# A two-layer adaptive feed-forward kernel: shared output tiles behind the expert blocks, weights in a ring of 14 slots, residual sums in the feed-forward

## The reference

```python
# layer 0: mix the channels of each batch element by a matrix chosen by its condition
xt = einsum('bct,bcd->bdt', x, W[condition])
# router: softmax scores over 16 experts, best 2 of 4 groups, top 2 experts -> gate
for e in 16 experts:   # width 128
    y += gate[e] * ((silu(xt @ ew1 + eb1) * (xt @ ew2 + eb2)) @ ew3 + eb3)
z = (silu(xt @ sw1 + sb1) * (xt @ sw2 + sb2)) @ sw3 + sb3      # shared expert, width 256
x = x + y + z
# layer 1: causal convolution of each channel with a kernel made from state-space parameters, masked by length
u = conv(x * mask, K) + x * mask * D,  masked again
h = relu(u @ up_w) ** 2
f = h @ down_w + ((u @ fc1_w) @ expert_w * (sum of top 2 of u @ gate_w)) @ fc2_w
x = x + layernorm(f) * gamma + beta
```

## Time and profile before

| | us |
|---|---|
| median of 3 runs | 416.92 |
| lowest, highest | 415.62, 421.37 |
| profiled execution, its own time | 415.92 |
| its span, first to last instruction | 413.9 |
| PE busy in it (1883 matmuls) | 343.5 |
| DVE, ACT, POOL busy | 182.1, 119.7, 93.7 |

### The profile page before, as it was taken

How to read it: one execution, slowest core, us unless ns; L and a number is a source line. 1 busy time by engine, 2 the same in 40 slices (tenths; PEclk the granted TensorE clock), 3 DMA queues, 4 the chain that set the end, 5 groups by cost and what they waited for, 6 DMA issues and landing times.

```text
span 413.9 us, 5243 instructions
## 1 busy us (share of the span) xinstructions
PE 343.5 (83%) x1883; PEld 248.5 (60%) x1883; DVE 182.1 (44%) x354; ACT 119.7 (29%) x199; POOL 93.7 (23%) x124
## 2 busy tenths in 40 slices
PE   8668999999969499799962316986999899999991
PEld 3235785568858488688721202442788778788871
DVE  2235886326816232133312563691432044542256
ACT  1255312013362123223200406345322233321222
POOL 3640003013413511521007773009200000000000
PEclk9889998899988889999987555996999999999998
DMA  6699302119999996757995765600000000110002
GB/s 227 225 364 406 105 0 50 54 51 333 385 396 404 408 338 229 258 181 187 379 348 135 230 244 187 220 2 0 2 0 0 2 0 2 51 51 2 1 0 102
DMA packets 34245, 67.85 MB, mean 164 GB/s; under 512 B 4584, under 2 KB 5580, under 8 KB 34220
## 3 DMA queue, kind: packets, MB, share of 16 engines
q1 hardware_dynamic: 28348, 52.79, 35.1%
q0 software_dynamic: 4112, 12.54, 10.1%
q10 hardware_dynamic: 1760, 2.20, 1.5%
HBM read 55.10 MB, written 12.40 MB: 163 GB/s over the span
## 4 chain that ended last, share of the span: by engine, by line
PE 64%; DMA 15%; DVE 7%; POOL 5%; issue 4%; ACT 3%; SPq 2%; DVEq 0%; POOLq 0%; ACTq 0%
PE bank L404 12%; PE bank L406 11%; PE bank L405 11%; PE bank L1405 9%; DMA ysort<-yout 6%; PE bank L1461 5%; PE bank L1394 4%; POOL yg L606 3%; PE bank L1365 3%; DMA xg<-xrow,tokx 2%; DVE acc L1154 2%; PE bank L1291 2%; PE bank L1379 2%; DMA xrow<-xstage 2%; DMA yg<-ysort,sloti 2%
## 5 line engine op out<-in xcount | busy, mean ns | idle before, releaser
L1405 PE MATMUL bank<-xt,ew 128*128 128x128 f32 x496 | 63.8, 284 | 0.0
L1405 PEld LDWEIGHTS bank<-xt,ew 128*128 128x128 f32 x496 | 61.1, 201 | 0.7 <-issue 0.5
L560 POOL DMA_INDIRECT xg<-xrow,tokx x31 | 32.7, 1055 | 88.7 <-PE bank L1365 52.2
L1394 PE MATMUL bank<-ew,bhid 128*128 128x512 f32 x62 | 32.8, 614 | 3.3 <-DVE yout L1101 3.3
L718 ACT ACTIVATE xt<-bank 128x512 f32<-128x512 f32 x31 | 18.4, 597 | 53.2 <-PE bank L1365 49.7
L1449 PE MATMUL bank<-ident,acc 128*128 128x128 f32 x32 | 8.9, 433 | 26.1 <-DVE acc L1154 26.1
L1217 DVE TENSOR_TENSOR sq<-rel 128x512 f32<-128x512 f32 x16 | 12.1, 758 | 41.1 <-ACT rel L804 41.0
L1365 PEld LDWEIGHTS bank<-ident,xg 128*128 128x128 f32 x124 | 15.9, 146 | 23.1 <-issue 13.8
L1101 DVE COPY yout<-bank 128x512 f32<-128x512 f32 x31 | 21.4, 691 | 16.4 <-DMA ysort<-yout 14.2
L1154 DVE SCALAR_TENSOR_TENSOR acc<-yg,gk,acc 128x512 f32<-128x512 f32 x16 | 18.2, 1150 | 21.1 <-DMA yg<-ysort,sloti 20.8
L404 PE MATMUL bank<-dnh,sqh 128*128 128x512 f32 x64 | 25.2, 394 | 2.5 <-DVE sql L1225 1.6
(11 more groups left out here) (302 smaller groups left out, 617.9 us busy)
## 6 DMA issues: line engine op xcount, KB each, us to landing
ew<-in_L_ffn_ew SPq DMA_DIRECT2D x24, 512.0 KB, 11.7
ew<-in_L_ffn_ew SPq DMA_DIRECT2D x45, 256.0 KB
ysort<-yout SPq DMA_DIRECT2D x31, 256.0 KB, 6.9
toep<-kpad SPq DMA_DIRECT2D x4, 1536.0 KB, 10.9
acc<-in_x SPq DMA_DIRECT2D x4, 512.0 KB, 5.3
xrow<-xstage ACTq DMA_DIRECT2D x4, 512.0 KB, 7.2
upraw<-in_L_ffn_up_w SPq DMA_DIRECT2D x1, 2048.0 KB, 11.1
dnraw<-in_L_ffn_down_w SPq DMA_DIRECT2D x1, 2048.0 KB, 9.2
```

What stands on the lines that cost most here:

```text
L560: pool.indirect_dma_start(xg[:, n % XGS, :], None, xrow, bass.IndirectOffsetOnAxis(ap=tokx[:, n:n + 1].bitcast(U32), axis=0))\
L1394: pe.matmul(bank[6 + n % 2][:, :], bhid[:, n % BHS, :], ew[:, ring(n), W3], start=True, stop=True)\
L1405: mm = pe.matmul(bank[2 + n % 2][:, w * P:(w + 1) * P], ew[:, ring(n), col + k * P:col + (k + 1) * P], xt[:, n % 2, k, :], start=(k == 0), ...
```

## The change

The shared output tiles move behind the 31 blocks: four of them come first, then each of the other four ahead of a transpose, and DVE's add_y calls go among the gathered adds. The third shared matrix and the hidden values get places of their own and are split in turns 21 to 24 of the block loops. ew becomes a ring of 14 slots; no expert weight is loaded before xrow is written, then experts 0 to 7, 12 and 13; experts 8 to 11 follow the last shared product; 17 further loads are spread by load_step. The Toeplitz pieces follow blocks 19 to 22. up_w is loaded after 13 gathered adds, gamma and beta after the last shared tile. POOL's residual sums stand behind its low parts. The product expert_w x fc2_w follows the convolution. In the last half of the tokens DVE does the centring, gamma, the scale and the residual in two operations that read the bank and acc, and ACT only the square root.

```diff
+    RING = 14
...
-        return n % E
+        return n if n < RING else n - RING if n < 2 * RING else n - 2 * RING + 8
...
+        if n < RING:
+            return ((st_in[0], 96), (st_in[1], 96), (st_in[3], 96), (st_in[2], 48))[n // 4]
+        return dyn_in[(n - RING) % DYN], 48 * ((n - RING) // DYN + 1)
+
+    def load_step(d):
+
+        return d * 7 // 5 if d < RING else d + 8
...
-        sp.dma_start(swraw[:, 2, :].rearrange("p (s n) -> p s n", s=SH),
-                     sw3.rearrange("(s p) n -> p s n", p=P)).then_inc(sraw_in, 16)
+        sp.dma_start(sw3raw[:, :].rearrange("p (s n) -> p s n", s=SH),
+                     sw3.rearrange("(s p) n -> p s n", p=P)).then_inc(l1_in, 16)
...
+            sp.dma_start(dst[:, :, W3], ew3[2 * g:2 * g + 2].rearrange("e p n -> p e n")).then_inc(landed, 16)
+
         sp.wait_ge(tr_done, 1)
         sp.dma_start(ewraw[:, :, :], expert_w.rearrange("(a p) m -> p a m", p=P)).then_inc(ew_in, 16)
-        for g in range(2, E // 4):
-            static_pair(g)
+        sp.wait_ge(tr_done, 2)
+        for par in range(2):
+            sp.wait_ge(xrow_out[par], 16 * NT // 4)
+        for g in range(4):
+            static_pair(g, st_in[g // 2])
+        static_pair(6, st_in[2])
         sp.dma_start(fcraw[:, :, :], fc1_w.rearrange("(k p) l -> p k l", p=P)).then_inc(l1_in, 16)
         sp.dma_start(fc2raw[:, :, :], fc2_w.rearrange("(a p) n -> p a n", p=P)).then_inc(l1_in, 16)
...
-        sp.wait_ge(y_done, NT)
-        for g in range(E // 4, E // 2):
-            static_pair(g)
-        for dst, src in ((gam, ln_gamma), (bet, ln_beta)):
-            sp.dma_start(dst[:, :], bass.AP(tensor=src.tensor, offset=0, ap=[[0, P], [1, T]])).then_inc(ln_in, 16)
+        sp.wait_ge(c_done, 2 * SH)
+        for g in range(4, 6):
+            static_pair(g, st_in[3])
...
-            if n < ND:
-                dynamic_load(n)
-            g = n - (E + TS * T // WCOLS - 1)
+            for d in range(NB - RING):
+                if load_step(d) == n:
+                    load(d)
+            g = n - 19
...
-        sp.wait_ge(comb_ok, YS)
+        sp.wait_ge(comb_ok, K * NT - 3)
         sp.dma_start(upraw[:, :, :], up_w.rearrange("(k p) m -> p k m", p=P)).then_inc(up_in, 16)
+        sp.wait_ge(y_done, NT)
+        for dst, src in ((gam, ln_gamma), (bet, ln_beta)):
+            sp.dma_start(dst[:, :], bass.AP(tensor=src.tensor, offset=0, ap=[[0, P], [1, T]])).then_inc(ln_in, 16)
...
-        pool.wait_ge(ln_in, 32)
-        for i in range(NT):
-            pool.wait_ge(xt_done, i + 1)
-            pool.tensor_tensor(acc[:, i, :], acc[:, i, :], bet[:, :], ALU.add).then_inc(resid_ok, 1)
         for j in range(JC):
             pool.wait_ge(dnh_ok, j + 1)
             pool.tensor_tensor(dnl[:, j, :], dnraw[:, j, :], f(dnh[:, j, :]), ALU.subtract).then_inc(dnl_ok, 1)
         pool.wait_ge(fch_ok, 1)
         pool.tensor_tensor(fcl[:, :, :], fcraw[:, :, :], f(fch[:, :, :]), ALU.subtract).then_inc(fcl_ok, 1)
+        pool.wait_ge(ln_in, 32)
+        pool.wait_ge(xt_done, NT)
+        for i in range(NT):
+            pool.tensor_tensor(acc[:, i, :], acc[:, i, :], bet[:, :], ALU.add).then_inc(resid_ok, 1)
...
-        split_hi(2)
...
-        def shared_hi(u):
-            act.wait_ge(hid_ok, u + 1)
-            act.activation(hidh(u), hid[:, u % 2, :], ACT.Copy).then_inc(hidh_ok, 1)
+            wait(act, hid_ok, u - 1)
+            act.activation(silu[:, u % 2, :], bank[4 + u % 2][:, :], ACT.Silu, bias=b12[:, 0, u % 2:u % 2 + 1])\
+                .then_inc(silu_ok, 1)
...
-        for par in range(2):
-            act.wait_ge(xrow_out[par], 16 * NT // 4)
-        shared_silu(0)
-        shared_silu(1)
-        shared_hi(0)
-        act.wait_ge(swl_ok, 3)
-        shared_silu(2)
-        shared_silu(3)
+        for u in range(4):
+            shared_silu(u)
...
-        for u in range(1, 4):
-            shared_hi(u)
...
+            if n == 21:
+                act.wait_ge(kpad_in, 32)
+                act.wait_ge(l1_in, 16 * 7)
+                act.activation(sw3h[:, :], sw3raw[:, :], ACT.Copy).then_inc(swh_ok, 1)
+            if n in (22, 23):
+                q = n - 22
+                act.activation(hidh[:, 2 * q:2 * q + 2, :], hid[:, 2 * q:2 * q + 2, :], ACT.Copy).then_inc(hidh_ok, 1)
...
-                    normalize(i)
...
-        split_lo(2)
...
-        shared_lo(0)
         shared_hid(1)
+        shared_hid(2)
         dve.wait_ge(tok_done, 1)
         dve.tensor_copy(tokx[:, :], bank[3][:, 0:NSLOT]).then_inc(tok_ok, 1)
-        shared_lo(1)
-        shared_hid(2)
         shared_hid(3)
-        shared_lo(2)
-        shared_lo(3)
...
-        for i in range(4, NT):
-            add_y(i)
...
+            elif n == 22:
+                dve.wait_ge(swh_ok, 3)
+                tt(sw3l[:, :], sw3raw[:, :], f(sw3h[:, :]), ALU.subtract).then_inc(swl_ok, 1)
+            elif n in (23, 24):
+                q = n - 23
+                dve.wait_ge(hidh_ok, q + 1)
+                tt(hidl[:, 2 * q:2 * q + 2, :], hid[:, 2 * q:2 * q + 2, :], f(hidh[:, 2 * q:2 * q + 2, :]), ALU.subtract)\
+                    .then_inc(hidl_ok, 1)
...
+        for i in range(4):
+            add_y(i)
         for n in range(K * NT):
             i, k = n // K, n % K
             dve.wait_ge(yg_in[n % YS], 16 * (n // YS + 1))
-            if n == 0:
-                dve.wait_ge(y_added, NT)
             if k:
                 dve.wait_ge(comb_ok, n)
+            else:
+                dve.wait_ge(y_added, i + 1)
             dve.scalar_tensor_tensor(acc[:, i, :], yg[:, n % YS, :], gk[:, k, i:i + 1], acc[:, i, :], ALU.mult,
                                      ALU.add).then_inc(comb_ok, 1)
+            if k and i + 4 < NT:
+                add_y(i + 4)
...
+        def centred(i):
+
+            if i == TH:
+                dve.wait_ge(fin_ok, TH)
+            dve.wait_ge(var_ok, i + 1)
+            dve.scalar_tensor_tensor(osum[:, i % TH, :], bank[i % TH][:, :], mv[:, i, 0:1], gam[:, :], ALU.subtract,
+                                     ALU.mult).then_inc(norm_ok, 1)
+
+        def scaled(i):
+
+            dve.wait_ge(std_ok, i + 1)
+            link(dve.reciprocal(rstd[:, i:i + 1], std[:, i:i + 1]))
+            dve.wait_ge(norm_ok, i + 1)
+            dve.wait_ge(resid_ok, i + 1)
+            dve.scalar_tensor_tensor(acc[:, i, :], osum[:, i % TH, :], rstd[:, i:i + 1], acc[:, i, :], ALU.mult,
+                                     ALU.add).then_inc(fin_ok, 1)
...
-                    scales(i)
-                    if i > TH:
-                        finish(i - 1)
-                finish(NT - 1)
+                    centred(i)
+                    scaled(i)
...
-        pe.wait_ge(l1_in, 16 * 6)
-        pe.wait_ge(swl_ok, 3)
-        for i in range(NT):
...
-            mm.then_inc(y_done, 1)
-            if i == NT - 3:
-                transpose_x(0)
-                transpose_x(1)
...
+        pe.wait_ge(hid_ok, 2 * SH)
+        transpose_x(0)
+        transpose_x(1)
...
-                if n == 2:
-                    pe.wait_ge(y_added, NT)
...
+                pe.wait_ge(gt_ok, 2)
...
-        pe.wait_ge(l1_in, 16 * 6)
+        def y_product(i):
+
+            q = i // TH
+            s = slice(i % TH * P, (i % TH + 1) * P)
+            dst = bank[4 + i % 4][:, :]
+            wait(pe, y_added, i - 3)
+            pe.matmul(dst, gt[:, i * P:(i + 1) * P], b3m[:, :], start=True, stop=False)
+            for part in range(SH):
+                w3 = slice(part * T, (part + 1) * T)
+                mm = split3(pe, dst, lambda k: (hidh[:, 2 * q + part, s], hidl[:, 2 * q + part, s]),
+                            lambda k: (sw3h[:, w3], sw3l[:, w3]), 1, start=False, stop=(part == SH - 1))
+            mm.then_inc(y_done, 1)
+
+        pe.wait_ge(l1_in, 16 * 7)
+        pe.wait_ge(kout_ok, 2)
         pe.wait_ge(yout_ok, NB)
-        for a in range(LC):
-            for m in range(LC):
-                mm = pe.matmul(bank[6 + a][:, :], ewt[:, m, a * P:(a + 1) * P], fc2raw[:, m, :],
-                               start=(m == 0), stop=(m == LC - 1))
-            mm.then_inc(m2_done, 1)
-        pe.wait_ge(kout_ok, 2)
+        pe.wait_ge(swl_ok, 3)
+        pe.wait_ge(hidl_ok, 2)
+        for i in range(4):
+            y_product(i)
         for i in range(NT):
+            if i + 4 < NT:
+                y_product(i + 4)
             pe.wait_ge(comb_ok, K * (i + 1))
-            wait(pe, u_ok, i - 5)
+            wait(pe, u_ok, i - 3)
             for k in range(KC):
-                mm = pe.transpose(bank[i % 6][:, k * P:(k + 1) * P], acc[:, i, k * P:(k + 1) * P], ident[:, :])
+                mm = pe.transpose(bank[i % 4][:, k * P:(k + 1) * P], acc[:, i, k * P:(k + 1) * P], ident[:, :])
             mm.then_inc(xt_done, 1)
...
+        pe.wait_ge(y_added, NT)
+        for a in range(LC):
+            for m in range(LC):
+                mm = pe.matmul(bank[6 + a][:, :], ewt[:, m, a * P:(a + 1) * P], fc2raw[:, m, :],
```

(2 more changed lines are left out.)

108 lines of the change are left out of this document (39 added, 69 removed).

## The result

The changed kernel takes 393.11 us (median of four runs, 392.07 to 399.43) against 416.27 for the kernel before on the same chip: a ratio of 0.945, 95% interval 0.941 to 0.949. The predicted 394 us was met, but by luck: large errors of opposite sign in the sum cancelled, and this part is mostly about them. Some executions of every kernel run at a lower mean granted clock and take longer (here 399.43 at 0.917, the other three 392.07 to 393.80 at 0.932 to 0.935); the ratios leave these out, the medians contain them.

A forecast was written before the change was run, and what follows sets the result against it. PE was taken to bound the path except at a preparation transfer, block stalls and the way to the convolution. Terms -20.3 + 0.1 - 12.7 + 1.5 - 2.1 + 12.7 - 1.2 = -22.0 gave 394 us from 415.92, range 378 to 402.

The forecast's parts named there:

- First block: Preparation to first block: without the xrow wait and shared output tiles, it starts near 72 us, 20.3 earlier (18 to 23).
- The blocks: First to last block: stalls removed and added nearly cancel, 16.4 us for 16.3, so the stage keeps its length.
- a restart at half clock costs 2.4: At the first block, after PE idles: running at half clock adds 2.4 us (0 to 3).
- behind gather 14: Second block stall, behind POOL's chain: 3.5 us wait plus 2.4 of half clock, 5.9 instead of 7.7 (1.4 to 8).
- behind the kpad writes: Third block stall, at gather 20: stays at 2.4 us.
- Load 14 lands some 2.2 us after block 28 could start, load 15 another 3.4 late: Last blocks: expert loads queued with Toeplitz pieces come late, adding 5.7 us (0 to 9).
- The first stall goes: Among the blocks, near block 7: the y copy's wait for a sorted write disappears, saving 6.2 us.
- Tail: Last block to convolution: earlier gathers and gathered adds at 0.75 us save 12.7 us (9 to 15).
- So sq of chunk 0 waits for all eight: Feed-forward: DVE's square waits for all eight POOL residual sums, 10.3 us plus 2.4 of half clock: +12.7 (1 to 14).
- sign of being wrong: Feed-forward: if sq stays under 2.5 us and PE does not stop, the largest cost is wrong.
- Rival 1: Feed-forward: POOL lets DVE in between two sums, costing 1 us instead of 12.7; total 382 us, chance 0.20.
- The end: Last four tiles: the fused DVE operations save 1.2 us (0.5 to 1.6).

The follow-up runs named there:

- the four extra sums: Changed kernel with four extra unused 128x512 GpSimd (POOL) sums behind its last combining gather, beside VectorE's last gathered adds: median 399.83 us, ratio 0.953.
- the run on the kernel before: Kernel before with only GpSimd's eight residual sums moved behind its splits in the feed-forward part: median 410.07 us against 416.44.
- the run with the gathers ahead: Changed kernel with gathers 14 to 16 moved ahead in GpSimd's queue and the kpad writes put behind gather 22: median 380.57 us, ratio 0.913.
- the kernel without waits for weights: Changed kernel with gathers ahead, VectorE's tail reordered, four products moved into the tail, late loads and Toeplitz pieces spread anew: median 370.17 us, ratio 0.894.

## Why the prediction came true, and where it was wrong

The time came out right by luck: errors of 10.3 us on one side met 13.8 on the other.

- **First block, -20.3 forecast, -18.3 measured.** The mechanism was right (xrow's wait gone, y tiles gone, gathers on full DMA); the gather started 0.7 us late and took 0.8 longer to land.
- **The blocks, +0.1 forecast, +6.1 measured.** The step "a restart at half clock costs 2.4" was put down at the first block, where it cost little: its products took 2.50 us instead of 1.95, and the third block starts 5.3 us behind the first. Where the half clock did cost, it was sized too small or left out: behind gather 14 (5.9 forecast with it, 7.1 measured), behind the kpad writes (2.4 forecast, 5.3 measured: 3.43 idle, then products of 3.25 us) and, left out, behind the late loads. "Load 14 lands some 2.2 us after block 28 could start, load 15 another 3.4 late" had the right total of idleness, 5.6 against 5.78, in one piece instead of two; with the half clock behind it the stall took 9.5 us against the 5.7 counted. "The first stall goes" was right.
- **Tail, -12.7 forecast, -10.4 measured.** First gather at 8.3 behind the last block (8.8 forecast), gathered adds at 0.75 throughout. Y tile 7 was ready 28.2 us behind the last block, as forecast (28.3), and eight adds behind it set the end, as forecast. What came late is the start of these eight, 30.9 instead of 29.0 behind the last block, because DVE was still busy with the late add of y tile 6; why that one was late is open. The residual sums' part in the gain was right: moving them alone gave 6.3 us of the tail.
- **Convolution to feed-forward, -0.6 forecast, -1.1 measured.** The logits did run at full clock as forecast.
- **Feed-forward, +12.7 forecast, about +0.3 measured. This is the step that failed.** "So sq of chunk 0 waits for all eight" took what one gathered add had suffered in the earlier trace rows for a rule of the two engines. It was true of that place, as the four extra sums show (6.08 us), and false in the feed-forward, where the engines take turns. The earlier trace rows could not tell: there sq overlapped a single POOL instruction with none behind it. The prediction's own sign of being wrong came true: sq stayed under 2.5 us (1.77) and PE hardly stopped. Rival 1 was right in mechanism; its 382 us were missed because the blocks and the tail took 8.3 us more than forecast. On the rule quoted in the prediction (the Trainium skill, "SBUF — State Buffer", section "SBUF: two separate sides"), that the port pair is taken for one instruction: the feed-forward agrees to 0.1 us, the tail contradicts it in two traces (5.31 and 6.08 us).
- **The end, -1.2 forecast, -2.0 measured** by undoing it. The mechanism was right.

By the table the errors are +2.0, +6.0 and +2.3 in the first three stretches and -0.5 and -13.3 in the last two: -3.5 together, of which 1.7 are lost again outside the span (2.0 us before, 3.7 after).

## What to carry to other kernels

Price a wait of TensorE at its idle time and again for the half clock behind it, here 1.9 to 3.7 us a time among the blocks; removing a wait for a transfer is worth it only if the bytes before it move to where the DMA engines have room, not to the next wait. In an in-order queue (GpSimd's gathers, VectorE's adds) put what others wait for ahead of what only has to be done some time. And a contention seen in one row is a fact of that place: look for a second row from where the change puts the work, or move that work alone, as the run on the kernel before did.

## What was not expected of the hardware

- A run of GpSimd sums held one VectorE instruction for 5.3 and 6.1 us in the tail, while in the feed-forward the engines alternate instruction by instruction, with both forms of VectorE's square. What decides between the two is not settled.
- SP's issue of a DMA took 3.5 us where 0.33 is usual, while the DMA engines moved 398 GB/s, and the next load went out behind it. That a full queue held the issue is a guess.
- In the run with the gathers ahead the granted clock stayed at 0.50 from 190 to 204 us with TensorE busy throughout. The changed kernel, with waits of much the same length before, had 1.00 at the same y tiles (197.5 to 208 us), and so had the kernel without waits for weights (176 to 190 us).
